# Attention block with adaptive layer norm: the first 512 rows normalised alone, and another order of the work up to the first scores

## The reference, cut to what matters

```python
mod = (silu(c) @ wmod).reshape(B, 6, 1, -1)          # c (2, 256), wmod (256, 1536)
sa, ca, ga, sb, cb, gb = ...                         # shift, gain and gate of both halves
ga = (2 * (ga >= 0) - 1) * maximum(abs(ga), 0.25)    # gb likewise
h = layernorm(x) * (1 + ca) + sa                     # x (2, 1024, 256)
q = (h @ Wq + bq) * DH ** -0.5;  k = h @ Wk + bk;  v = h @ Wv + bv    # 16 heads of 128
q = q * cos + rotate_half(q) * sin                   # k likewise
attn = softmax(where(causal, -max, q @ k.T))
x = x + ga * ((attn @ v) @ Wo + bo)
h = layernorm(x) * (1 + cb) + sb
x = x + gb * down(silu(gate(h)) * up(h))             # weights (int - 128) * scale, 704 hidden
```

## Time and profile before

| | us |
|---|---|
| timed runs, median (lowest, highest) | 970.99 (970.98, 971.55) |
| profiled execution, its own time | 968.9 |
| its span in the trace | 967.0 |
| TensorE busy in the span | 934.2 (97%) |
| VectorE, ScalarE, GpSimd busy | 735.9, 673.4, 774.9 |

### The profile page before, as it was taken

How to read it: one execution, slowest core, us unless ns; L and a number is a source line. 1 busy time by engine, 2 the same in 40 slices (tenths; PEclk the granted TensorE clock), 3 DMA queues, 4 the chain that set the end, 5 groups by cost and what they waited for, 6 DMA issues and landing times.

```text
span 967.0 us, 20178 instructions
## 1 busy us (share of the span) xinstructions
PE 934.2 (97%) x5667; PEld 833.6 (86%) x5667; DVE 735.9 (76%) x1582; ACT 673.4 (70%) x1354; POOL 774.9 (80%) x555
## 2 busy tenths in 40 slices
PE   6989999999999999999999999999999999878898
PEld 5878998888889989989998888889989989767787
DVE  6766877778878877787877877887878777867544
ACT  5766766677677767676767677777777676757763
POOL 2468988898898988898889888998889888795653
PEclk9999999999999999999999999999999999999999
DMA  7554554554445545554455554644555545531011
GB/s 256 163 137 137 179 166 142 159 182 154 140 136 175 167 136 158 179 167 150 145 156 174 169 150 133 183 148 139 156 170 168 158 147 171 177 95 44 1 44 46
DMA packets 108978, 141.63 MB, mean 146 GB/s; under 512 B 12948, under 2 KB 80084, under 8 KB 108884
## 3 DMA queue, kind: packets, MB, share of 16 engines
q1 hardware_dynamic: 108884, 140.72, 48.5%
HBM read 62.36 MB, written 44.76 MB: 111 GB/s over the span
## 4 chain that ended last, share of the span: by engine, by line
PE 87%; DVE 3%; POOL 3%; issue 2%; ACT 2%; DMA 1%; SPq 0%; POOLq 0%; DVEq 0%; ACTq 0%
PE ps_r L1565 18%; PE ps_r L1564 18%; PE ps_r L1563 18%; PE ps_s L1563 7%; PE ps_s L1565 7%; PE ps_s L1564 7%; PE ps_t L1728 5%; PE ps_s L1570 1%; PE ps_s L1573 1%; PE ps_r L1570 1%; PE ps_r L1572 1%; PE ps_r L1668 1%; ACT probs L1046 1%; POOL pT_lo L782 1%; DMA wmod_a<-in_L_wmod 1%
## 5 line engine op out<-in xcount | busy, mean ns | idle before, releaser
L1046 ACT ACTIVATE probs<-ps_s,neg_max 128x128 f32<-128x128 f32 (+7 forms) x256 | 189.8, 742 | 84.5 <-DVE neg_max L1451 82.3
L764 POOL TENSOR_TENSOR swapped<-swapped,sin_sb 128x512 f32<-128x512 f32 x124 | 161.2, 1300 | 94.4 <-DMA swapped<-straight 94.1
L1451 DVE CUSTOM_DVE_ANT_0 ps_s<-ps_s,mask_wide 128x128 f32<-128x128 f32 (+7 forms) x256 | 193.6, 756 | 14.8 <-PE ps_s L1565 12.4
L782 POOL TENSOR_TENSOR pT_lo<-side_p,pT_hi 128x1024 fp32r<-128x1024 f32 (+2 forms) x93 | 195.3, 2131 | 0.7 <-ACT pT_hi L1035 0.7
L773 POOL TENSOR_TENSOR qk_lo<-swapped,qk_hi 128x512 fp32r<-128x512 f32 x124 | 159.4, 1297 | 19.7 <-ACT qk_hi L930 19.6
L767 POOL TENSOR_TENSOR swapped<-swapped,qk_cos 128x512 f32<-128x512 f32 x124 | 161.3, 1301 | 10.5
L1563 PE MATMUL ps_s<-qk_hi 128*128 128x512 f32 (+4 forms) x384 | 142.1, 370 | 2.4 <-ACT probs L1046 2.3
L1379 DVE STREAM_TRANSPOSE squares<-probs 128x1024 f32<-128x1024 f32 (+2 forms) x93 | 103.1, 1109 | 51.6 <-ACT probs L1046 48.4
L1565 PE MATMUL ps_r<-pT_hi,v_lo 128*128 128x512 f32 (+3 forms) x384 | 133.0, 346 | 0.0
L1564 PE MATMUL ps_r<-pT_lo,v_hi 128*128 128x512 f32 (+3 forms) x384 | 132.6, 345 | 0.0
L1565 PE MATMUL ps_s<-qk_hi,qk_lo 128*128 128x512 f32 (+4 forms) x384 | 131.4, 342 | 0.0
(11 more groups left out here) (205 smaller groups left out, 2409.3 us busy)
## 6 DMA issues: line engine op xcount, KB each, us to landing
swapped<-straight SPq DMA_DIRECT2D x252, 128.0 KB, 2.7
side_out<-squares SPq DMA_DIRECT2D x31, 512.0 KB, 2.6
side_p<-side_out SPq DMA_DIRECT2D x124, 128.0 KB, 2.9
side_out<-squares SPq DMA_DIRECT2D x31, 448.0 KB, 2.6
side_p<-side_out SPq DMA_DIRECT2D x124, 112.0 KB, 2.6
side_out<-squares SPq DMA_DIRECT2D x31, 384.0 KB, 2.3
side_p<-side_out SPq DMA_DIRECT2D x124, 96.0 KB, 2.2
x_in<-in_L_attn_x SPq DMA_DIRECT2D x4, 512.0 KB, 5.6
```

The source lines that it names most:

```text
L764: pool.tensor_tensor(swapped[:, q, :], swapped[:, q, :], sin_sb[:, at_], ALU.mult).then_inc(rotated, 1)
L782: pool.tensor_tensor(turned_at(t, 0, t + 1)(pT_lo).rearrange("p k (i c) -> p k i c", c=SQUARE), from_squares(side_p[t], t)[:, t::-1, :, :] ...
L1046: nc.scalar.activation(halved(t, probs[:, P_AT[step] * P:(P_AT[step] + t + 1) * P]), score_rows(step, t), ACT.Exp, bias=neg_max[:, t:t + 1 ...
L1451: nc.vector.tensor_tensor_reduce(rows, rows, halved(t, mask_wide[:, SEQ - n_keys:SEQ]), -1.0, -MASKED, ALU.add, ALU.min, accum_out=neg_max ...
```

## The change

Eight things change, all before unit 0; nothing in the loop does.

1. SyncE issues the second part of the input behind the first two parts of the modulation weights, and the weights of keys and queries before the biases.
2. VectorE normalises the first four tiles (512 rows) to the end, then takes the moments of the next four, then the gains, then the roots of these four, two `h_low`, and only then normalises the second four.
3. The query bias and `wq_low` come behind that, and the moments of the third and fourth part of the input behind `wq_low`: of the third before `h_low(2)`, of the fourth before `h_low(3)`.
4. ScalarE takes the roots in three portions of 4, 4 and 8 tiles, writes the key weights' high part before the modulation copy and the query weights' behind `h_out(1)`.
5. ScalarE takes K0 out of PSUM between `h_out(1)` and `h_out(2)`, Q0 behind `h_out(3)`, then the value weights' high part.
6. TensorE turns the first 512 rows, does the bias columns and makes K0 before it turns the second 512 rows; two warm matmuls stand behind the first turn and three behind the bias columns, five in all and not six, and none behind the last two turns.
7. VectorE does `cosine(1)` before the second `v_low`, and `first_low(1)` before the third `qk_add`.
8. ScalarE does the first `qk_high` before the first two `whiten`, and the second before the next two.

```diff
             load_x(0)
-            load_x(1)
             load_mod(0, 0, wmod_a_ready)
             load_mod(1, 1, wmod_a_ready)
+            load_x(1)
+            load_w(WK, 0)
+            load_w(WQ, 0)
...
-            roots(1, slice(0, NTT // 2))
+            roots(1, slice(0, NTT // 4))
+            act.wait_ge(raw_ready[WK], 16)
+            w_high(WK)
             act.wait_ge(mod_made, 1)
             mod_out(0, ps_s[:, 1, :])
+            roots(2, slice(NTT // 4, NTT // 2))
+            act.wait_ge(gain_ready, 1)
+            h_out(0)
+            h_out(1)
+            act.wait_ge(raw_ready[WQ], 16)
+            w_high(WQ)
             col_out(0, COL_C, 2, ps_s[:, 0, COLS_BANK[1]:SEQ])
...
+            qk_out(first, FIRST_QK[0])
+            h_out(2)
+            h_out(3)
+            qk_out(first, FIRST_QK[1])
...
-            norm(x_in, lambda t: xn[:, t, :], range(NTT // 2), lambda n: dve.wait_ge(x_ready[n], 16), xn_ready)
+            norm(x_in, lambda t: xn[:, t, :], range(NTT // 4), x_landed, xn_ready)
+            moments(x_in, range(NTT // 4, NTT // 2), x_landed)
...
+            reciprocal_roots(range(NTT // 4, NTT // 2))
...
+            h_low(0)
+            h_low(1)
+            normalise(x_in, lambda t: xn[:, t, :], range(NTT // 4, NTT // 2), xn_ready)
...
+            for n in range(2, 4):
+                dve.wait_ge(x_ready[n], 16)
+                for t in range(4 * n, 4 * n + 4):
+                    last = nc.vector.bn_stats(bn[:, t, :], x_in[:, t, :])
                 h_low(n)
...
             qk_add(first, FIRST_QK[0])
+            cosine(1)
             v_low(first, FIRST_V[1])
-            cosine(1)
...
-            for n in range(GROUPS4 // 2):
-                turn_xn(n)
-                warm((1, 2, 2, 1)[n])
+            turn_xn(0)
+            warm(2)
+            turn_xn(1)
+            pe.wait_ge(b_rows_ready, 48)
+            turn_rows(b_rows, 3 * HEADS, ps_s[:, 0, COLS_BANK[1]:COLS_BANK[1] + 3 * HEADS])
+            warm(3)
             pe.wait_ge(w_ready[WK], 1)
-            for n, piece in enumerate(FIRST_QK):
-                pe.wait_ge(hT_ready, KT * (n // 2) + KT)
-                make(Span(0, 0), piece)
+            pe.wait_ge(hT_ready, KT)
+            make(Span(0, 0), FIRST_QK[0])
+            turn_xn(2)
+            turn_xn(3)
+            make(Span(0, 0), FIRST_QK[1])
+            pe.wait_ge(hT_ready, 2 * KT)
+            make(Span(0, 0), FIRST_QK[2])
+            make(Span(0, 0), FIRST_QK[3])
```

36 lines of the change are left out of this document (11 added, 25 removed).

## The result

The changed kernel takes 976.32 us (median of 6 runs, 975.08 to 977.08), the kernel before, on the same chip, 971.01 us (6 runs, 969.81 to 971.56). The ratio is 1.0052, 95% interval [1.0042, 1.0062]. The forecast was slower by 1.9 us, 972.9 us, with a range up to 975.0: it had the direction right and the size too small.

What follows compares the result with a forecast made beforehand. TensorE, busy 97% of the span, was taken as the bound, with the start chain releasing the loop. K1 1.95 us later less 0.1 gave 1.85, rounded to 1.9: 970.99 + 1.9 = 972.9 us, range 970.6 to 975.0.

Steps and rivals of the forecast that it cites:

- They land at 6.5 instead of 7.99 us: Start of the kernel: modulation weights land 1.5 us sooner, with 0.52 MB less ahead of them at 320 GB/s.
- nothing gained: Bound on the modulation weights' landing: they still land at 7.99 us; the other bound was near 6.1.
- K0 at 15.45: TensorE's keys of the first rows: K0 starts at 15.45 us and not at 17.22, 1.75 us gained.
- K1 at 22.0, 1.95 us later: K1 on TensorE waits for VectorE's fourth low part of h: 22.0 instead of 20.04 us, bounds 1.5 and 3.4.
- I take 0.1 back: VectorE and GpSimd taking turns from K1 to the last rotary sum: 0.1 us regained, sum ends at 36.3 us.
- TensorE's own way ... level with ScalarE's: TensorE's path through V3, second modulation product and scores reaches 42.9 us against ScalarE's 43.0, with no slack left.
- K1 to the exponentials: -0.1: Stretch from K1 to the second tile's exponentials: 0.1 us of the 1.95 regained, exponentials at 43.0 us.
- A shift of the exponentials goes through to the end one to one: The delay of the second tile's exponentials, 1.85 us from 41.12 us, reaches the kernel's end undiminished.
- Rival (a): TensorE's clock falls behind the idle time before K1, or rises later at K0: 974.4 us, chance 0.25.
- (b): Half absorbed, as VectorE and GpSimd get out of each other's way: +0.5 to +1, 971.8 us, chance 0.15.
- (c): Keys of the first rows come 1.75 us earlier, the rest is hidden, loop starts sooner: 968.6 us, chance 0.09.
- (d): Hidden altogether, a later chain sets the loop's entry: no change, 971.0 us, chance 0.06.

Runs made afterwards that it cites:

- mods_ahead: The changed kernel with the biases ahead of the key and query weights again, modulation weights still ahead of the second part of x; 976.6 us, ratio 1.0055.
- after_again: The changed kernel profiled once more, nothing altered; span of the profiled execution 973.6 us.
- loads_alone: The kernel before with only SyncE's new order of the first transfers; 974.97 us, ratio 1.0051.
- warm_mods: The changed kernel with 8 unused matmuls of 512 columns spread through the second modulation product; 976.23 us, ratio 1.0052.
- late_undone: The changed kernel with the old late order of VectorE and ScalarE (items 7 and 8 undone); 976.03 us, ratio 1.0046.
- delay_k1: The kernel before with 7 more moment instructions on VectorE ahead of the fourth low part of h; 973.07 us, ratio 1.0024.
- late_alone: The kernel before with items 7 and 8 only (late order of VectorE and ScalarE); 971.8 us, ratio 1.0016.
- tight: The changed kernel with all four h in one go, all moments behind them and VectorE's old late order; 976.85 us, ratio 1.0061.

## Why the prediction was wrong, step by step

**"They land at 6.5 instead of 7.99 us" failed.** In eleven profiled executions with the new order (or mods_ahead's) the first modulation matmul began between 7.42 and 9.25 us, median 8.21; in nine with the old between 7.82 and 8.47, median 8.12. The 1.5 us were 0.52 MB divided by the rate of the stretch, and they aren't there: the second block of the modulation weights landed at 7.3 to 9.1 us. In three of the eleven it began 0.3 to 0.8 us later than in the latest of the nine. All of K0 and K1 was counted from it; it puts K0 and K1 0.9 us later in the profile of the changed kernel and 1.7 in the second one (8.32 against 6.6). The forecast named "nothing gained" as a bound of the landing, but the bounds of K1's lateness, 1.5 and 3.4 us, were not worked out with it.

**K0 at 15.45** was 15.98 and 16.84. From modulation start to K0 8.5 us passed, as against 8.85 in the forecast: the steps were right, their start wrong.

**"K1 at 22.0, 1.95 us later"** was 22.41 and 23.25, 2.4 and 3.2 later. Its mechanism stood: K1 waits for VectorE's fourth low part, behind a ScalarE that has K0 to take out first and behind two groups of moments, idle 2.54 us against 2.4 to 2.5. From the modulation start it took 14.95 us, forecast 15.4; that this step was shorter hid part of the late start, by luck. The bound that was named for K0 at 1.2 GHz (1.2 and 0.4 us) was met at K0, with up to 1.5 us at K1, in 3 of 7 executions.

**"I take 0.1 back"** was right in its mechanism, and it did not matter. GpSimd's sine products of K1 and Q1, against the earlier trace rows:

```profile
27.76 1.29 POOL L793 TENSOR_TENSOR swapped_b<-swapped_b,sin_sb 128x512 f32<-128x512 f32 x1 [1.74 <-DMA swapped_b<-straight_b]
30.85 1.83 POOL L793 TENSOR_TENSOR swapped_b<-swapped_b,sin_sb 128x512 f32<-128x512 f32 x1 [1.80 <-DMA swapped_b<-straight_b]
```

The sum of K0 ended 0.54 us behind the first of them (29.59 against 29.05 us; forecast 28.5 for GpSimd's end, with K1 0.4 us sooner). The second was to be over by 31.0 us and wasn't until 32.68, and `first_low(0)` (31.43 us) waited for it. The last rotary sum ended at 37.08 us, 14.67 behind K1 where it had been 14.40: 0.3 us more, not 0.1 less. In after_again it stood 13.9 us behind K1 and in mods_ahead 14.2, so the sign changes from one execution to the next; the exponentials came 22.9 us behind K1 in all three, so they did not hang on it. In the experiments a VectorE step of 0.17 us became one of up to 1.28 in this way. That is the rule of the Trainium skill, page "SBUF — State Buffer", section "Who interferes with whom", that the blocked engine waits for the other's whole instruction; the trace agrees.

**"TensorE's own way ... level with ScalarE's" failed in size, and with it "K1 to the exponentials: -0.1".** V3 was forecast 8.4 us behind K1 and was 8.56. But the second modulation product was priced at 3.75 us and took 5.2, since the clock fell within it and not at its end; the scores and keys behind it took as long as before. From its own rows TensorE's way reads 37.97 + 5.6 + 1.35 = 44.9 us, and exp came at 45.29 (the row maximum was in at 45.20, and ScalarE's two passes of h, which wait for turns on TensorE, ended just then). The exponentials of the first tile, on ScalarE's own way, were 3.0 us late (40.56 against 37.53); TensorE's way became the bound: +1.8 us from K1 to exp, in three profiles of the changed order (22.9 against 21.1). The starts give the terms: K1 to the second product 10.34 us instead of 9.13 (V3's wait, +1.2), the product up to the scores 5.08 instead of 3.59 (the clock, +1.5), from the scores to exp 7.46 instead of 8.36 (the slack, -0.9). loads_alone has the second term without the first, and exp stands 21.6 us behind K1, 0.5 more than before; warm_mods has the first without the second, and it is 0.2 more, with its eight matmuls counted in. So it took both to use up the slack and cost 1.8. The forecast had seen that the slack of about 1 us was gone, and then priced the next thing on that way as in the old trace.

**"A shift of the exponentials goes through to the end one to one" was right for the medians.** The table shows it for fourteen kernels within 1.2 us. Between two single traces it does not hold: beside the profile of the kernel before, the lateness grew behind exp by 0 to 1.9 us up to the idle time of the earlier trace rows and by 0.1 to 2.8 us from there to the end, in all other kernels' profiles. Since both profiles of the kernel before are faster than every one of its timed executions beside the experiments (969.6 to 972.7 us), some of that growth may stand in those too; this is open.

So the sum up to the exponentials reads: forecast 1.95 - 0.1 = 1.85; measured 3.2 + 1.8 = 5.0 in after_again, 2.4 + 1.8 = 4.2 in the first profile; the medians differ by 5.3. Two terms failed: the landing that moved K1, and K1 to the exponentials.

**Rival (a)**, the clock (974.4 us), was the nearest. It was placed between K0 and V0, and there the lower clock was met in 4 of 7 profiles with the changed order and no matmuls put in ahead of K1: at K0 in three, and in late_undone just as forecast, behind the idle time of 2.54 us ahead of K1, at a price of 1.4 us. In the other six the matmuls behind that idle time kept their 0.23 us, as in delay_k1 behind 1.74 us. In every profile with the changed late order and no matmuls put in, the fall within the second modulation product came instead or on top. Its price was right (1.5 us); that it could act behind V0 too was left out. (b), (c) and (d) fell: nothing was absorbed.

**Open.** What sets whether the clock falls within the second modulation product or behind it isn't settled: late_alone suggests V3's idle time, but loads_alone and late_undone had none there, and it fell within the product too. Nor is it settled why the same idle time is followed by a fall in one execution and not in the next: 2.54 us ahead of K1 (late_undone against the changed kernel), 2.94 us at 870 us (the changed kernel against the kernel before). How the 5.3 us divide over a typical timed execution isn't either, since the transfers and the clock differ from one to the next; only the sum agrees. Why the second block of modulation weights took up to 3.6 us behind the first was not tried. No version beat the kernel before: the chain of VectorE up to K1 had 0.9 us of idle time, and every rearrangement of it made K1 later or, as in tight, moved the wait from K1 to V2.

## What to carry to other kernels

Splitting a batch to start its first half sooner pays only if the engine that does the splitting has slack behind it; here VectorE was busy almost without a break up to the operand of K1, and the second set of roots and the first half's consumers went in front of the second half. Count a chain from the event that really releases it, and give the landing of a transfer the spread of several executions, not bytes over rate. When a shift uses up the slack of another path, price that path anew with each of its clocked stretches at the worse level. And compare traces at the same mark in the program before comparing spans: two executions of one kernel can differ at a place that the change didn't touch.

## What the runs showed of the hardware that was not expected

- One queue, the same order of the first three transfers: the first modulation matmul, which waits for the last of 1 MB, began at 7.42 to 9.25 us in eleven executions; where it waited for the last of 1.5 MB, at 7.82 to 8.47 us in nine.
- TensorE's matmuls of 512 columns stood 0.43 us apart at K0 in three profiles whose clock column shows 1.00 in that stretch; the kernel before has the same column at 12.77 to 15.70 us with its warm matmuls 0.43 us apart. Early in the span the spacing of matmuls has to be read, not that column.
- A VectorE step on 128x8 elements took 0.17 us alone and 1.19 to 1.28 us beside GpSimd's 128x512 products.
- The same idle time of TensorE, of about 2.9 us near 870 us, was followed by 3.4 or 6.8 us at 1.2 GHz in 13 profiles and by none in 7; the one of 2.5 us ahead of K1 was followed by 3.4 us of it in late_undone and by none in the changed kernel.
